# Two blocks of a decoder on one core: new orders of steps, and second copies of five small buffers

## What is computed

```python
# block 0: x is the stream, ctx the context
normed = x * rsqrt(mean(x**2) + 1e-6) * norm_w
attn = softmax(split(normed @ wq) @ split(ctx @ wk).T)       # 16 heads of 64
x = x + merge(attn @ split(ctx @ wv)) @ wo
# block 1: the same stream, ctx again for its cross attention
h = mha(ln(x, g1, b1), ln(x, g1, b1), causal=True);  x = x + h @ m_proj_w + m_proj_b
h = mha(ln(x, g2, b2), ctx, causal=False);           x = x + h @ c_proj_w + c_proj_b
x = x + relu(ln(x, g3, b3) @ f_w1 + f_b1) @ f_w2 + f_b2
```

## Time and profile before

| | us |
|---|---|
| median of three runs | 5389.3 |
| the three runs | 5389.18, 5389.30, 5392.09 |
| the profiled execution | 5392.09 |
| its span, first to last instruction | 5390.3 |
| PE busy in the span | 4841.2 (90%) |
| ACT busy | 3940.5 (73%) |
| DVE busy | 3103.8 (58%) |
| POOL busy | 530.0 (10%) |
| mean granted clock of TensorE | 0.975 of full |

### The profile page before, as it was taken

The page is one execution under the profiler, slowest core; times in us unless marked ns, Lnnn a source line. Parts: engine busy times, 40 slices in busy tenths (PEclk is TensorE's granted clock), DMA queues, the critical chain, the costliest instruction groups (busy, mean ns, idle before and its releaser), DMA issues. The chain is left out here.

```text
span 5390.3 us, 143424 instructions
## 1 busy us (share of the span) xinstructions
PE 4841.2 (90%) x47160; PEld 3984.0 (74%) x47160; DVE 3103.8 (58%) x8003; ACT 3940.5 (73%) x16437; POOL 530.0 (10%) x845
## 2 busy tenths in 40 slices
...
DMA packets 219920, 181.12 MB, mean 34 GB/s; under 512 B 111313, under 2 KB 203921, under 8 KB 219857
## 3 DMA queue, kind: packets, MB, share of 16 engines
...
...
## 5 line engine op out<-in xcount | busy, mean ns | idle before, releaser
L934 ACT ACTIVATE ps<-ps,negmax 128x77 f32<-128x77 f32 (+2 forms) x6144 | 2063.1, 368 | 475.4 <-DVE negmax L1184 474.9
L934 ACT ACTIVATION_READ_ACCUMULATOR ps<-ps,negmax 128x1 f32 x6144 | 1465.2, 245 | 0.0
L1184 DVE TENSOR_REDUCE negmax<-ps 128x4 f32<-128x308 f32 (+2 forms) x1792 | 928.3, 564 | 283.7 <-PE ps L1522 150.7
L886 POOL TENSOR_TENSOR small<-small 128x1 f32<-128x1 f32 (+1 forms) x448 | 255.3, 570 | 4728.0 <-DVE small L1161 2442.7
L1179 DVE TENSOR_TENSOR zTl<-ps,zTh 128x256 fp32r<-128x256 f32 x512 | 204.6, 419 | 517.6 <-ACT zTh L914 517.4
L1028 ACT ACTIVATE probs<-ps 128x512 f32<-128x512 f32 x768 | 399.1, 617 | 117.3 <-PE ps L1574 117.2
L914 ACT COPY probs<-ps 77x512 f32<-77x512 f32 x512 | 287.6, 591 | 202.9 <-PE ps L1536 198.7
L914 ACT CAST zTh<-ps 128x256 fp32r<-128x256 f32 x512 | 190.9, 407 | 224.1 <-PE ps L1609 155.5
L1397 PE MATMUL ps<-ident,z 128*128 128x128 f32 x768 | 140.7, 291 | 225.8 <-DVE z L1170 161.0
L1493 PE MATMUL ps<-k0bd,q0T 128*128 128x154 f32 x2048 | 339.7, 298 | 1.4 <-ACT q0T L914 0.8
L1389 PE MATMUL ps<-zTh,hi_f 128*128 128x256 f32 x1024 | 321.6, 314 | 5.2 <-issue 1.9
(11 more groups left out here) (227 smaller groups left out, 12982.5 us busy)
## 6 DMA issues: line engine op xcount, KB each, us to landing
keys_of<-kring SPq DMA_DIRECT2D x128, 154.0 KB, 1.9
k0bd<-keys_of SPq DMA_DIRECT2D x128, 154.0 KB, 3.2
...
```

The source lines that it names most:

```text
L886: nc.gpsimd.tensor_tensor(rstd[:, stage, ts], veps[:, stage, ts], minus_half[:, ts], ALU.pow).then_inc(rstd_ready[stage], 1)
L934: ins = nc.scalar.activation(scores, scores, ACT.Exp, bias=negmax[w][:, t, h:h + 1], accum_out=sums[w][:, t, h:h + 1])
L1184: nc.vector.tensor_reduce(dst, bank(s)[:, 0:heads * width].rearrange("p (h k) -> p h k", h=heads), AX_X, ALU.max, negate=True).then_inc(ma ...
```

## The change

Five kinds of buffer get more copies, so that steps of neighbouring batches or of the two attentions no longer share them: `q1T` (one for each attention), `maxT` and `logs` (likewise), `negmax` and `sums` (a third of each, for the cross attention alone), and `aTh`/`aTl` (the results of `pv`, which were kept in `zTh`/`zTl`). `rows` of the tile t = 1 get a space of their own instead of `q0T`'s. The three tables of the loop, and those of the end of the head and of the tail, are written anew in another order and with other banks. No product, exponential or transfer is added or taken away. Ahead of all its work PE passes 34 idle waits instead of 10.

```diff
 LOOP_ORDER_TEXT = """
-rms+ pv.1.1:6 proj.1.0:6 stat.2.0 tr0.1.1-:3 qs0.1.3-:7 tr0.0.0-:4 norm.2.0 qs0.0.2-:6 proj.1.1:5
-pv0.1-:3 tr0.1.0-:2 qs0.1.2-:1 stat.2.1 norm.2.1 turn.2.0:6 turn.2.1:5 tr0.1.3-:0 pv0.0-:2 q1.2:5
-norm.0+ turn.0+:3 tr0.0.2-:4 tr0.1.2-:0 tr0.0.3-:6 qs2.1:2541 pv0.3-:0 pv0.2-:3 q0.2+:7 qs2.0:6230 wo.0-:4
-stat.1.0- norm.1.0- wo.1-:5 stat.1.1- q0.1+:4 ln.2 q0.0+:3 norm.1.1- mt.2:5 turn.1.0-:2 turn.1.1-:6
-sk2.0:5170 sk2.1:6432 k1-:5 q1.1-:1 pv.2.0:2 pv.2.1:7 qsB.1-:6501 proj.2.1:3 proj.2.0:6 stat.3.0
-qsB.0-:0347 v1-:1 norm.3.0 turn.3.0:6 stat.3.1 norm.3.1 turn.3.1:1 qsA-:5437 ln.1-
...
+ln.2 rms+ skA.1:6015 qs0.1.3-:4 pv0.0-:3 pv0.1-:2 pv.1.1:7 turn.0+:0 tr0.0.2-:5 proj.1.0:7 proj.1.1:4 tr0.1.2-:7
+tr0.1.3-:6 q0.0+:4 turn.2.0:1 tr0.0.3-:0 turn.2.1:6 pv0.2-:5 q1.2:6 pv0.3-:1 qs2.1:0647 qs2.0:5321 wo.0-:0 stat.2.0
+wo.1-:7 q0.1+:0 stat.2.1 turn.1.0-:5 q0.3+:3 norm.2.0 stat.1.0- turn.1.1-:4 stat.1.1- qs0.0.1+:7 mt.2:1 k1-:3
+sk2.0:0164 sk2.1:3725 q1.1-:4 pv.2.0:3 pv.2.1:6 stat.3.0 qsB.1-:5147 v1-:2 proj.2.0:6 qsB.0-:3052 qs0.0.0+:7
+proj.2.1:6 q0.2+:1 turn.3.0:6 qsA-:4352 turn.3.1:6 qs0.1.1+:7 h.3:6 h.2:0 norm.1.0- norm.2.1 h.0:2 norm.1.1-
...
-        q1T = sb("q1T", [P, KT, T])
+        q1T = [sb("q1T0", [P, KT, T])]
...
-        negmax = [sb(f"negmax{i}", [P, TT, H]) for i in range(2)]
-        sums = [sb(f"sums{i}", [P, TT, H]) for i in range(2)]
-        logs = sb("logs", [P, TT, H])
+        negmax = [sb(f"negmax{i}", [P, TT, H]) for i in range(3)]
+        sums = [sb(f"sums{i}", [P, TT, H]) for i in range(3)]
+        logs = [sb(f"logs{i}", [P, TT, H]) for i in range(2)]
...
-        rows0 = sb("rows0", [P, 2, 4 * S])
+        q1T += [sb("q1T1", [P, KT, T])]
+        maxT = [sb(f"maxT{i}", [P, T], F32R) for i in range(2)]
+        aTh, aTl = sb("aTh", [P, KT, T], F32R), sb("aTl", [P, KT, T], F32R)
+        rows0 = [sb(f"rows0_{i}", [P, 2, 4 * S]) for i in range(TT)]
...
         def rows_of_four(t, g):
-            if t == 0:
-                return rows0[:, g % 2, :]
-            return q0T[:, 2 * g:2 * g + 2, :].rearrange("p a q -> p (a q)")[:, 0:4 * S]
+            return rows0[t][:, g % 2, :]
...
-                return zTh[:, step[2]:step[2] + 1, :], zTl[:, step[2]:step[2] + 1, :], 1, T
+                return aTh[:, step[2]:step[2] + 1, :], aTl[:, step[2]:step[2] + 1, :], 1, T
...
-            for _ in range(10):
+            for _ in range(34):
                 pe.wait_ge(consts_made, 9)
```

More of the change, by code:

```diff
@@ L64 @@
[L64 to L68, removed]
+skA.1/3 skA.1/2 skA.1/0 skA.1/1 qs0.1.3 pv.1.1 turn.0 tr0.0.2 pv0.0 tr0.1.2 tr0.1.3 q0.0 turn.2.0 turn.2.1 pv0.1
@@ L69 @@
+pv0.2 tr0.0.3 q1.2 pv0.3 qs2.1/0 qs2.1/3 qs2.0/2 qs2.0/3 qs2.0/1 qs2.0/0 qs2.1/2 qs2.1/1 turn.1.0 q0.1 ln.2 turn.1.1
+q0.3 mt.2 qs0.0.1 k1 sk2.0/3 sk2.0/0 sk2.0/1 sk2.0/2 sk2.1/0 sk2.1/3 sk2.1/1 sk2.1/2 q1.1 pv.2.1 pv.2.0 qsB.1/0 v1
+qsB.1/2 qsB.1/3 qsB.1/1 qsB.0/2 qsB.0/0 qsB.0/3 turn.3.0 qs0.0.0 qsB.0/1 turn.3.1 qsA/3 qsA/1 qsA/0 qsA/2 q0.2 ln.1
+tr0.0.0 tr0.0.1 mt.1 qs0.1.1 qs0.1.0 skB/2 skB/3 skB/1 skB/0 qs0.0.3 skA.0/0 skA.0/3 tr0.1.1 tr0.1.0 skA.0/2 skA.0/1
+qs0.1.2 qs0.0.2 pv.1.0
 """
 DVE_ORDER_TEXT = """
-rms pv.1.1 proj.1.0 stat.2.0 qs0.1.3/0 qs0.0.2/0 norm.2.0 proj.1.1 stat.2.1 qs0.1.3/1 qs0.0.2/1 norm.2.1
@@ L72 @@
[L72 to L76, removed]
@@ L77 @@
-qs0.1.0/1 qs0.0.3/1 pv.1.0 f2.1
+rms qs0.1.3/0 norm.0 qs0.1.3/1 pv.1.1 turn.0 proj.1.0 stat.2.0 proj.1.1 stat.2.1 norm.2.0 norm.2.1 turn.2.0 turn.2.1
+pv0.2 pv0.1 pv0.0 qs2.1/0 qs2.1/3 pv0.3 qs2.1/1 qs2.1/2 qs2.0/2 qs2.0/3 qs2.0/0 qs2.0/1 wo.0 stat.1.0 norm.1.0 wo.1
+stat.1.1 norm.1.1 turn.1.0 ln.2 turn.1.1 qs0.0.1/0 qs0.0.1/1 pv.2.1 pv.2.0 qsB.1/0 qsB.1/2 qsB.1/1 qsB.1/3 proj.2.0
+stat.3.0 qsB.0/2 qsB.0/0 norm.3.0 qsB.0/3 proj.2.1 qs0.0.0/0 stat.3.1 qsB.0/1 turn.3.0 norm.3.1 qs0.0.0/1 qsA/3
+turn.3.1 qsA/1 qsA/0 qsA/2 h.3/0 qs0.1.1/0 h.3/1 h.2/0 h.0/0 h.2/1 ln.1 h.0/1 h.1/0 qs0.1.0/0 qs0.0.3/0 h.1/1
@@ L78 @@
+qs0.1.1/1 qs0.1.0/1 qs0.0.3/1 f2.0 qs0.1.2/0 f2.1 qs0.0.2/0 qs0.1.2/1 qs0.0.2/1 pv.1.0
 """
@@ L178 @@
 """
 TAIL_ORDER_TEXT = """
[L180 to L190, removed]
@@ L196 @@
-turn.2.0@2:6 norm.2.1@2 turn.2.1@2:0 q1.2@2:5 qs2.0@2:2741 qs2.1@2:3605 ln.2@2 mt.2@2:4 sk2.1@2:7125 sk2.0@2:3604
-pv.2.0@2:2 pv.2.1@2:7 proj.2.0@2:1 proj.2.1@2:4 stat.3.0@2 norm.3.0@2 stat.3.1@2 turn.3.0@2:3 norm.3.1@2
-turn.3.1@2:0 h.2@2:5 h.0@2:6 h.1@2:2 h.3@2:7 f2.0@2:1 f2.1@2:4
+rms@2 ln.1@2 skA.1@0:3065 stat.2.0@0 qs0.1.3@1:1 pv0.0@1:7 tr0.1.2@1:5 pv.1.1@0:0 pv0.1@1:7 ln.2@2 proj.1.0@0:3
+tr0.0.3@1:0 proj.1.1@0:6 tr0.1.3@1:2 tr0.0.2@1:0 turn.0@2:1 stat.2.1@0 pv0.3@1:4 turn.2.0@0:3 turn.2.1@0:0 pv0.2@1:6
@@ new lines @@
+q1.2@0:5 q0.1@2:3 qs2.0@0:6150 stat.1.0@1 wo.0@1:7 stat.1.1@1 qs2.1@0:0524 wo.1@1:3 q0.0@2:7 qs0.0.1@2:0
+turn.1.0@1:2 qs0.0.0@2:5 norm.2.0@0 mt.2@0:7 turn.1.1@1:6 sk2.1@0:3421 k1@1:7 norm.2.1@0 sk2.0@0:3251 stat.3.0@0
+pv.2.1@0:0 qs0.1.1@2:4 stat.3.1@0 q1.1@1:7 pv.2.0@0:5 qsB.1@1:2736 tr0.0.0@2:1 proj.2.0@0:0 qsB.0@1:1045
+proj.2.1@0:3 qsA@1:3620 q0.3@2:7 qs0.1.0@2:1 turn.3.1@0:7 turn.3.0@0:4 q0.2@2:5 norm.1.0@1 v1@1:6 h.3@0:4 h.2@0:7
+tr0.1.1@2:0 tr0.0.1@2:6 mt.1@1:3 h.1@0:2 norm.3.0@0 skB@1:3650 h.0@0:4 skA.0@1:5210 qs0.1.3@2:7 tr0.1.0@2:3
```

170 lines of the change are left out of this document (84 added, 86 removed).

## The result

The changed kernel takes 5174.7 us (median of 4 runs, 5167.2 to 5182.7), against 5389.4 before: a ratio of 0.960 [0.958, 0.962], 215 us saved. The forecast was 5140, 35 us too low, with 5050 to 5330 as its range. The profiled execution of after took 5167.2 us.

A forecast was written before the change was run, and what follows sets the result against it. PE bounds the kernel, idle 549 us in queue-latency waits. Busy 69.26 plus 4.3 us waiting makes a 73.6 us turn against 77.74: 4.1 us times 61 saves 252 us, giving 5140 us, range 5050 to 5330.

The forecast's parts named there:

- What goes: PE's old waits ahead of turn.3, turn.2.0, proj.1.0 and proj.2.0: about 5.2 of 5.8 us a turn disappear.
- 1, low part of `pv0.3`: PE waits 0.6 us ahead of wo.0 for DVE's low part of pv0.3, behind both qs2 steps.
- 2, `qs0.0.1`: Behind two wo steps, PE waits 0.25 us for q0.1's result, queued on ACT behind the qs2 exponentials.
- 3, `mt.2`: mt.2 on PE waits 0.35 us for ln.2, which passes through ACT and then DVE.
- 4, bank of `k1` in `sk2.1`: sk2.1 on PE waits 0.95 us for bank 3, held until ACT copies k1; the largest wait, and new.
- 5, small ones: Waits at qs0.0.0, qsA, turn.3.1 to h.3, proj.1.0, q0.0, q1.2 and qs2.1: together 2.15 us a turn.
- The clock: Full clock expected in nearly every turn, since idle time in any 12 us is at most about 1.6 us; counted as nothing.
- The head and the tail: New orders at the end of the head and in the tail: 0 us, with 15 us either way.
- The waits did not come back: Rival: new waits are 6.4 us, not 4.3, and the clock drops in most turns for 0.9 us; 5320 us, chance 0.26.
- The case of better cover: Rival: the small later waits in a turn are covered, the turn is 71.5 us; 5010 us, chance 0.10.
- The case of no change: Rival: none of the waits hangs on the order, transfers or contention set the turn; 5390 us, chance 0.04.
- The jump back: Rival: PE waits 4.40 us for its instructions at each loop jump; 5408 us, chance 0.10 including any other loss.

The follow-up runs named there:

- e4: The changed kernel with turn.3.1 put back directly behind turn.3.0 on PE, ahead of qsA: 5310.8 us, 0.984 of before.
- e12: The changed kernel with proj.1.0 and proj.1.1 put back directly behind pv.1.1 on PE: 5305.4 us, 0.984 of before.
- e1: The changed kernel's code and buffer copies with the old tables of orders and ten idle waits: 5398.1 us, 1.001 of before.
- e6: The changed kernel with six needless repeats of a qs2.0 product where PE waits for coTl: 5105.4 us, 0.946 of before.
- e2: The changed kernel with 10 idle waits of PE ahead of its work instead of 34: 5179.7 us, 0.961 of before.
- e8: The changed kernel with 64 idle waits ahead of ACT's loop, to move its code in memory: 5168.4 us, 0.957 of before.
- e9: The changed kernel with 64 idle waits ahead of VectorE's loop, to move its code in memory: 5165.4 us, 0.958 of before.

## Why the prediction came out as it did

**What goes.** Right. Of the 5.8 us of the earlier trace rows I counted 5.2 as gone; in the turn below no wait is left at `turn.3`, `proj.1.0` and `proj.2.0`, and at `turn.2` 0.36 of 1.0. e4 and e12 show the two largest moves at work, and e1 that the copies give nothing alone.

**The length of a turn at full clock.** Forecast 73.6, measured 73.70. Part of this is luck: PE idles 3.86 us where I had 4.3, and is busy for 69.84 where I took the 69.26 of the earlier trace rows. All of PE's waits in the turn of after from 1067.17, in order of time:

```profile
1068.11 1.07 PE L1593 MATMUL ps<-probs,v 128*32 128x256 f32 x16 [0.39 <-ACT probs L1018]
1073.59 0.38 PE L1380 MATMUL ps<-xTh,hi_wq 128*128 128x256 f32 x1 [0.34 <-DVE xs L1288]
1076.28 0.44 PE L1388 MATMUL ps<-ident,z 128*128 128x128 f32 x2 [0.36 <-DVE z L1160]
1082.61 0.79 PE L1494 MATMUL ps<-kcbd,q1T 32*128 32x154 f32 x10 [1.22 <-DVE coTl L1169]
1095.09 0.38 PE L1380 MATMUL ps<-z1Th,hi_mk 128*128 128x256 f32 x1 [0.16 <-ACT q0T L904]
1098.89 0.57 PE L1537 MATMUL ps<-maxT,head_of 32*77 32x256 f32 x8 [0.86 <-ACT k1bd L949]
1109.42 0.79 PE L1484 MATMUL ps<-k0bd,q0T 128*128 128x154 f32 x4 [0.17 <-ACT ps L924]
```

By the points of the walk:

| point | forecast | measured |
|---|---|---|
| 1, low part of `pv0.3` | 0.6, at `wo.0` | 1.22, inside `qs2.0` |
| 2, `qs0.0.1` | 0.25 | none |
| 3, `mt.2` | 0.35 | 0.2 in some turns, none in this one |
| 4, bank of `k1` in `sk2.1` | 0.95 | 0.86 |
| 5, small ones | 2.15 | 1.4: `pv.1.1` 0.39, `turn.2.1` 0.36, `q0.0` 0.34, `qs0.0.0` 0.17, `k1` 0.16 |

Point 4 was the one that a walk finds well: one queue, one bank, rows for every piece. Point 1 had the right VectorE work in the right order (two maxima, then the low part), but I looked for its reader and not for the bank that it reads. `qs2.0` takes that bank for its last piece, ahead of `wo.0`. Of point 5 the bank of `proj.1.1` ahead of `q0.0` came as forecast (0.34 against 0.35), and the one ahead of `qs0.0.0` at 0.17 instead of 0.4. I also listed `qsA`, `turn.3.1` and `h.3` with 1.0 us, which do not show, and missed `pv.1.1` on ACT's exponentials and what is left at `turn.2.1`.

**The clock.** This is the step that failed. I took the full clock in nearly every turn and nothing for its drops, because the most idle time in 12 us of my walk was 1.6 us. With the mean turn at 74.75 and one at full clock at 73.72, the drops cost 1.0 us a turn, 62 us in 60 turns. e6 gives about the same by taking the longest wait away: its sixty turns take 67 us less, and its median is 69 us lower. My 1.6 was also too little: point 1 stood in the walk at 0.6 and not at 1.22, and the 0.36 at `turn.2.1` not at all. In a turn PE waits 0.34, 0.36 and 1.22 us within 10 us, and in the turns of the long kind the clock falls 0.6 to 1.1 us behind the end of the last. By two of my own signs this part was wrong: the clock still drops in most turns, and PE's busy time is 70.9 us a turn on average and not 69 to 70.

The Trainium skill ("TensorE: Matmul & The Clock Gate", Part 1: The HAM clock gate (the "warmup" mystery)) ties the clock to how busy TensorE has been kept. The trace agrees in direction: in all 43 turns the drop stands behind the cluster of waits, and filling one of them keeps the clock. It does not tell which turn falls. Turns with like waits differ. Why one in four is spared in after, and in before, and why these stand in rows, stays open.

**The head and the tail.** I took 0 with 15 us either way. They gave 46 us: 25.8 up to the first `f2.1` that ends a turn, and 20.2 behind the last. VectorE's step `f2.1` in time, before and then after, in the first turn and sixty turns on: 492.35 and 5156.26; 466.59 and 4951.61. The 60 turns between took 4663.9 and 4485.0, so 178.9 of the 224.9 us are theirs. Of the 46 us, 25 are idle time of PE and 21 busy time, and the granted clock is higher: 0.97 against 0.90 from 320 us to the first of these points, and 0.89 against 0.85 behind the last. So there was more to win here than to lose, and part of it is the clock again. Which of the new orders of head and tail bring it was not tested.

The sum closes: 7 us for a full turn that is 0.1 longer, 62 for the clock, 4 for the sixty-first turn, whose saving I had counted and which these sixty leave out, and 46 less for head and tail make 27 us over my 5140; the profiled execution lies at 5167. That the total came within 35 us is in part luck: two terms that I had at nothing were wrong by 62 and 46 us, in opposite directions.

**The rivals.** The waits did not come back (3.8 us, not 6.4), but the other half of that rival did: the clock drops in most turns, at 1.0 us on average where it said 0.9. The case of better cover is out. The case of no change is out by the result, and e4 and e12 show that waits hang on the order. The jump back is the interesting one. The instruction queue has 325 packets (2.66 MB) in the trace of after and 26 (0.21 MB) in that of before: five are fetched in every turn of after, and in before none comes between 474 and 5155 us. But no wait of PE at the start of a turn is put down to it. The Trainium skill ("Runtime: NRT & Kernel Launch", Instruction fetch mechanics) says that a taken branch to a place outside the pages held stops the engine until that page has come; no such stop could be seen here. Which engine fetches, and what it would cost on an engine without slack, stays open after e2, e8 and e9.
